# POOL drains three times inside the last stage of a transformer kernel

## The chip, the cores and the metric

The kernel runs on one core of a Trainium2 chip. The metric is the device time in microseconds (us) of one execution. The core has five engines with an instruction queue each: TensorE (PE, matmuls into PSUM), VectorE (DVE), ScalarE (ACT), GpSimd (POOL) and SyncE (SP, which here only issues DMAs). They run on their own and meet through semaphores: an instruction can raise one, and another queue can stand still until it has reached a value.

## The reference

Two layers, each with attention and a feed-forward part, over x of 4 x 512 tokens with 512 columns:

```python
x = x + _L0_xattn_ref(_layernorm(x), token_ids, ...)   # 4 experts chosen by token id
x = x + _L0_ffn_ref(_layernorm(x), norm_w, w_gv, w_out)  # quantised gated FFN, 2048 wide
x = x + _L1_xattn_ref(_layernorm(x), ctx, Wq, Wg, bg, Wkv, Wo)  # linear attention, 16 heads
x = x + _L1_ffn_ref(_layernorm(x), gate_w, w_gate, w_up, w_down, sw_gate, sw_up, sw_down)
```

The last part is a mixture of 16 experts. Each token goes to its 4 best, an expert takes at most 256 tokens, and a shared network runs for all:

```python
xg = xpad[buf]                        # 16 x 256 gathered rows
mid = silu(xg @ w_gate) * (xg @ w_up)
eout = mid @ w_down * wbuf[..., None]
y = zeros.at[buf.reshape(-1)].add(eout)[:T]
shared = silu(x @ sw_gate) * (x @ sw_up) @ sw_down
return y + shared
```

## The kernel before, in words

The kernel has two blocks. A block gives each engine its own list of instructions; at its end every engine drains and all meet in a barrier. The first block (`front_experts0`) does the first layer's attention part, the token-id experts, and ends near 235 us. The second (`ffn0_to_experts1`) does all the rest. Between and after them, the callback of `semaphores` (lines 94 and 95) clears the block's semaphores on POOL, with a drain ahead, and holds another barrier. In the profile the closing of the first block carries line 231 and that of the second line 1395.

The change touches the last part of the second block, `shared_experts1`, and there POOL's list `gpsimd`. Tokens are worked on in tiles of 128 rows and 512 columns (256 KB); an expert has two such tiles.

- POOL's `body` is called when its other work (statistics of the norms, and one half of splitting the shared network's weights, line 3629) is over. It waits for `found_ready`: DVE has then found out which token sits in which slot of which expert (`gather_idx`, `scatter_idx`, line 3989).
- `fetch(e)` issues two gathers (line 3639): 128 rows of the normed x from HBM into `xg`, by indirect DMA. TensorE transposes them.
- `add(e)` waits until the additions of the expert before have landed (`added`, lines 3644 and 3646), because two experts may add to the same row; grants ACT the other pair of output tiles (`y_free`, line 3647); then waits for each tile of `e_y` and issues a scatter that adds it to `out` in HBM (line 3651, an indirect DMA too).
- `body` runs `fetch(e + 2)` and `add(e)` for the 16 experts. It starts with `fetch(0)` and `fetch(1)` and a wait until the shared result stands in `out` (line 3660), and ends with a wait for the last additions (line 3666). Experts 14 and 15 are the last two; no fetch comes with them.
- ACT's `body` makes `e_y` from PSUM with the slots' weights (line 3746), behind waits for `y_free` and for the matmuls.
- TensorE runs each expert's matmuls in three float32r products (lines 54 to 56). SP loads the experts' weights.

POOL's DMAs of the whole kernel are: in the first block the stores of summaries (line 307) and the gathers of x (line 314), in the second the gathers by the tokens' place (line 1464), and those of lines 3639 and 3651. POOL issues them in program order, among its compute instructions.

Of the kernel before, what the change touches and what calls it, by code (L numbers as in the profile page):

```python
# [10 lines left out]
P = 128  # L11
# [756 lines left out]


def front(nc, g, io):  # L770


    ctx = ExitStack()
    with ctx:
        def sb(name, shape, dt):
            return ctx.enter_context(nc.sbuf_tensor(name, shape, dt))

        sem = semaphores(nc, ctx, "f")


        ctx_raw = sb("ctx_raw", [P, KD, S], fp32)
        ctx_h = sb("ctx_h", [P, KD, S], f32r)
        ctx_l = sb("ctx_l", [P, KD, S], f32r)
        wkv_raw = sb("wkv_raw", [P, KD, 2 * D], fp32)
        wkv_h = sb("wkv_h", [P, KD, 2 * D], f32r)
        wkv_l = sb("wkv_l", [P, KD, 2 * D], f32r)
        kneg = [sb(f"kneg{n}", [P, D], fp32) for n in range(2)]
        kexp = kneg
        kf = [sb(f"kf{n}", [P, D], fp32) for n in range(2)]
        k_h = sb("k_h", [P, 4, D], f32r)  # L790
        k_l = sb("k_l", [P, 4, D], f32r)
        v_h = sb("v_h", [P, 4, D], f32r)
        v_l = sb("v_l", [P, 4, D], f32r)
        summ = sb("summ", [P, 2, KD, P], fp32)
        summ_h = sb("summ_h", [P, 2 * KD * P], f32r)
        summ_l = sb("summ_l", [P, 2 * KD * P], f32r)
        wchunk = [sb(f"wchunk{n}", [P, 1024], fp32) for n in range(3)]
        wsum = sb("wsum", [P, 24], fp32)
        wtot = sb("wtot", [P, 2], fp32)
        wall = sb("wall", [P, 2], fp32)  # L800
        tok = sb("tok", [P, TT], i32)
        tokf = sb("tokf", [P, TT], fp32)
        ge = sb("ge", [P, TT, E0 - 1], fp32)
        mask = sb("mask", [P, TT, E0], fp32)
        mask_b = sb("mask_b", [P, TT, E0], bf16)
        tot = sb("tot", [P, TT, E0], fp32)
        rank = sb("rank", [P, TT, E0], fp32)
        inc = sb("inc", [P, TT, E0], fp32)
        cnt_i = sb("cnt_i", [P, E0], i32)
        ntile = sb("ntile", [P, E0], fp32)  # L810
        upto = sb("upto", [P, E0], fp32)
        base = sb("base", [P, E0], fp32)
        base_rows = sb("base_rows", [P, E0], fp32)
        tex = sb("tex", [1, 3, SORTED + AHEAD], fp32)
        posf = sb("posf", [P, TT], fp32)
        qi = sb("qi", [P, 2, TT], i32)
        qf = sb("qf", [P, 2, TT], fp32)

        hot_row = wkv_raw[:, 0:2, :].rearrange("p a (t n) -> p (a t) n", n=P)
        hot_tile = wkv_raw[:, 2, 0:TT * (SORTED + AHEAD)].rearrange("p (t n) -> p t n", t=TT)  # L820
        idxf = sb("idxf", [P, SORTED + AHEAD], fp32)

        s = {n: sem(n) for n in (
            "tok_in wkv_in wkv_hi wkv_lo mask_ready counted rank_read hot_ready sorted_ready route_step "
            "ctx_in ctx_hi ctx_lo ctx_kept ctx_raw_free ctx_used "
            "k_ready v_ready kbank_free vbank_free kneg_ready kexp_ready kf_ready k_hi k_lo v_hi v_lo "
            "kv_used bd_ready ks_ready summ_taken summ_ready summ_hi summ_lo summ_out "
            "wsum_ready wtot_ready wall_ready wscale_ready last_step").split()}
        w_in = [sem(f"w_in{n}") for n in range(3)]
        w_free = [sem(f"w_free{n}") for n in range(3)]  # L830

        kbank, vbank = g.bank[0:2], g.bank[2:4]
        bd_bank, ks_bank, route_bank, sort_bank = g.bank[4], g.bank[5], g.bank[6], g.bank[7]
        NJ = SORTED + AHEAD

        with nc.Block() as block:
            @block.sync
            def _(sp):
                sp.dma_start(tok[:, :], io["tokens"]).then_inc(s["tok_in"], 16)
                sp.dma_start(wkv_raw[:, :, :], io["wkv"]).then_inc(s["wkv_in"], 16)  # L840
                with sp.Fori(0, B) as b:
                    sp.wait_ge(s["ctx_raw_free"], b + 1)
                    sp.dma_start(ctx_raw[:, :, :], io["ctx"][:, bass.ds(b, 1), :, :].rearrange("p a k s -> p (a k) s")).then_inc(s["ctx_in"], 16)
                    for c in range(6):
                        sp.wait_ge(w_free[c % 3], at(b, 2, c // 3))
                        sp.dma_start(wchunk[c % 3][:, :], io["wffn"][:, bass.ds(b * 6144 + c * 1024, 1024)]).then_inc(w_in[c % 3], 16)

            @block.gpsimd
            def _(gp):
                gp.wait_ge(s["wtot_ready"], 1)  # L850
                gp.partition_all_reduce(wall[:, :], wtot[:, :], P, bass.bass_isa.ReduceOp.add).then_inc(s["wall_ready"], 1)

            @block.scalar
            def _(act):
                act.wait_ge(s["wkv_in"], 16)
                act.activation(wkv_h[:, :, :], wkv_raw[:, :, :], ACT.Copy).then_inc(s["wkv_hi"], 1)
                for n in range(3):
                    act.sem_inc(w_free[n], 1)
                with act.Fori(0, B) as b:
                    act.wait_ge(s["ctx_in"], (b + 1) * 16)  # L860
                    act.wait_ge(s["ctx_used"], b + 1)
                    act.wait_ge(s["ctx_kept"], b * 32 + 32)
                    act.activation(ctx_h[:, :, :], ctx_raw[:, :, :], ACT.Copy).then_inc(s["ctx_hi"], 1)

                    for part, mine, every in (("ctx_hi", ctx_h, g.ctx_h), ("ctx_lo", ctx_l, g.ctx_l)):
                        act.wait_ge(s[part], b + 1)
                        act.dma_start(f(every[:, bass.ds(b, 1), :].rearrange("p a n -> p (a n)")),
                                     f(mine[:, :, :].rearrange("p k n -> p (k n)"))).then_inc(s["ctx_kept"], 16)
                    for t in range(4):
                        for c in ((0, 1), (2, 3), (4,), (5,))[t]:  # L870
                            act.wait_ge(w_in[c % 3], at(b, 2, c // 3) * 16)
                            act.activation(wchunk[c % 3][:, :], wchunk[c % 3][:, :], ACT.Abs,
                                           accum_out=wsum[:, bass.ds(b * 6 + c, 1)]).then_inc(w_free[c % 3], 1)
                        if t == 0:
                            act.wait_ge(s["kv_used"], b + 1)
                        act.wait_ge(s["kneg_ready"], at(b, 4, t))
                        act.activation(kexp[t % 2][:, :], kneg[t % 2][:, :], ACT.Exp).then_inc(s["kexp_ready"], 1)
                        act.wait_ge(s["v_ready"], at(b, 4, t))
                        act.activation(v_h[:, t, :], vbank[t % 2][:, :], ACT.Copy).then_inc(s["v_hi"], 1)
                        act.wait_ge(s["kf_ready"], at(b, 4, t))  # L880
                        act.activation(k_h[:, t, :], kf[t % 2][:, :], ACT.Copy).then_inc(s["k_hi"], 1)
                    act.wait_ge(s["summ_ready"], b + 1)
                    act.wait_ge(s["summ_out"], b * 32 + 32)
                    act.activation(summ_h[:, :], summ[:, :, :, :].rearrange("p w k n -> p (w k n)"), ACT.Copy).then_inc(s["summ_hi"], 1)
                    for part, (ready, mine) in enumerate((("summ_hi", summ_h), ("summ_lo", summ_l))):
                        act.wait_ge(s[ready], b + 1)
                        act.dma_start(g.summ_dram[bass.ds(b, 1), part, :, :].rearrange("a p n -> (a p) n"), f(mine[:, :])).then_inc(s["summ_out"], 16)
                act.wait_ge(s["summ_out"], 32 * (B + 1))
                act.wait_ge(s["ctx_kept"], 32 * (B + 1))

            @block.tensor
            def _(pe):

                pe.wait_ge(s["mask_ready"], 1)
                m2 = mask_b[:, :, :].rearrange("p t e -> p (t e)")
                pe.matmul(route_bank[:, 0:TT * E0], g.before_b[:, :], m2, start=True, stop=True)
                pe.matmul(route_bank[:, 256:256 + TT * E0], g.ones_b[:, :], m2, start=True, stop=True).then_inc(s["counted"], 1)

                pe.wait_ge(s["hot_ready"], 1)
                for t in range(TT):  # L900
# [1351 lines left out]


def ffn0(nc, g, io):

    PAIRS = TT // 2
# [1928 lines left out]
```

## Time and profile before

| what | us |
|---|---|
| median of 3 runs | 1107.89 |
| lowest and highest of them | 1104.54, 1109.40 |
| the profiled execution | 1107.26 |
| its span, first to last instruction | 1105.5 |
| PE busy | 1048.1 (95%) |
| DVE busy | 673.4 (61%) |
| ACT busy | 591.9 (54%) |
| POOL busy | 281.9 (26%) |

The span is measured by the hardware profiler in one execution. Times in the views are us from the start of the span. "Busy" leaves out what an engine's sequencer does alone: semaphore waits, branches and drains. Such records carry a q behind the engine's name (POOLq). A DMA that POOL issues counts as a POOL instruction, as long as POOL works at issuing it; its landing is later.

### The profile page before, as it was taken

How to read it: one execution, taken by the hardware profiler on the slowest of the kernel's cores; microseconds unless marked ns; L12 is line 12 of the kernel's file. 1: busy time of each engine (PE TensorE's matmuls, PEld its weight loads, DVE VectorE, ACT ScalarE, POOL GpSimd, SP SyncE). 2: the span in 40 equal slices, each digit the busy share in tenths (PEclk: the TensorE clock that was granted, in tenths of full speed). 3: DMA queues.
4: the chain of work that ended last, by engine and by line, in shares of the span. 5: the costliest groups of instructions: out<-in, count | busy, mean ns of one | idle time of the engine just before them, and what ended most of it. 6: DMA issues, size and time to landing. Idle time of an engine off the chain costs nothing.

```text
span 1105.5 us, 16228 instructions
## 1 busy us (share of the span) xinstructions
PE 1048.1 (95%) x5830; PEld 824.7 (75%) x5830; DVE 673.4 (61%) x1226; ACT 591.9 (54%) x890; POOL 281.9 (26%) x445
## 2 busy tenths in 40 slices
PE   7999999979999999989999999899899999999994
PEld 5887777766455555568888888688687899999993
DVE  6746555435998998665655655466823666666660
ACT  5765787734898898853333244121113466666651
POOL 1012222113555553100000034100010044444442
PEclk9999999989999999999999999999999999999998
DMA  6682666521100000201111232302043588888853
GB/s 213 227 303 97 172 173 188 163 68 59 30 20 20 30 20 11 97 1 68 48 58 51 101 108 77 100 29 77 1 152 111 181 236 223 225 227 230 231 132 39
DMA packets 47606, 127.03 MB, mean 115 GB/s; under 512 B 5810, under 2 KB 6834, under 8 KB 46772
## 3 DMA queue, kind: packets, MB, share of 16 engines
q1 hardware_dynamic: 36516, 97.53, 26.1%
q0 software_dynamic: 10448, 27.58, 11.0%
q10 hardware_dynamic: 576, 1.05, 0.3%
q8 instruction: 40, 0.66, 0.2%
q14 instruction: 26, 0.21, 0.1%
HBM read 97.76 MB, written 28.38 MB: 114 GB/s over the span
## 4 chain that ended last, share of the span: by engine, by line
PE 67%; DVE 5%; ACT 3%; issue 2%; POOL 1%; DMA 0%; ACTq 0%; DVEq 0%; POOLq 0%
PE bank L54 16%; PE bank L55 15%; PE bank L56 15%; PE bank L1819 9%; PE bank L1840 4%; PE bank L3812 1%; PE bank L1831 1%; DVE s_hot_tile L3975 1%; PE bank L1913 1%; PE bank L1895 1%; DVE s_pick L3972 1%; PE bank L1924 1%; PE bank L1849 1%; PE bank L1923 1%; DVE s_mid L3999 0%
## 5 line engine op out<-in xcount | busy, mean ns | idle before, releaser
L1819 PE MATMUL bank<-w,f_qT 128*128 128x512 bf16 x512 | 117.9, 379 | 0.2 <-DVE f_h L2060 0.2
L3651 POOL DMA_INDIRECT out<-e_y,scatter_idx x32 | 69.0, 2157 | 115.7 <-ACT e_y L3746 111.5
L1819 PEld LDWEIGHTS bank<-w,f_qT 128*128 128x128 bf16 x512 | 48.7, 98 | 50.8 <-issue 0.6
L3688 ACT ACTIVATE s_m_h<-s_mid 128x512 fp32r<-128x512 f32 (+1 forms) x24 | 15.1, 631 | 126.9 <-DVE s_mid L3999 76.3
L3639 POOL DMA_INDIRECT e_xg<-xn_rows,gather_idx x32 | 33.7, 1054 | 172.6 <-DVE gather_idx L3989 105.7
L54 PE MATMUL bank<-wkv_h,ctx_h_all 128*128 128x512 f32 x128 | 54.0, 422 | 12.0 <-DVE wkv_l L708 7.4
L1840 PE MATMUL bank<-w,f_q2T 128*128 128x512 bf16 x256 | 59.5, 387 | 2.4 <-ACT f_q2T L1593 2.4
L54 PE MATMUL bank<-e_xT_h,e_wg_h 128*128 128x256 f32 (+1 forms) x192 | 56.5, 294 | 2.9 <-issue 2.1
L2060 DVE SCALAR_TENSOR_TENSOR f_h<-bank,f_columns,f_sg 128x512 f32<-128x512 f32 x64 | 47.9, 749 | 13.8 <-ACT f_sg L1577 6.8
L4077 DVE TENSOR_TENSOR e_mid<-bank,e_sil 128x256 f32<-128x256 f32 (+1 forms) x48 | 20.3, 423 | 55.5 <-ACT e_sil L3720 55.4
L55 PE MATMUL bank<-e_xT_l,e_wu_h 128*128 128x256 f32 (+1 forms) x192 | 54.1, 282 | 0.0
L56 PE MATMUL bank<-e_xT_h,e_wg_l 128*128 128x256 f32 (+1 forms) x192 | 54.0, 281 | 0.0
L55 PE MATMUL bank<-e_xT_l,e_wg_h 128*128 128x256 f32 (+1 forms) x192 | 54.0, 281 | 0.0
L56 PE MATMUL bank<-e_xT_h,e_wu_l 128*128 128x256 f32 (+1 forms) x192 | 54.0, 281 | 0.0
L54 PE MATMUL bank<-e_xT_h,e_wu_h 128*128 128x256 f32 (+1 forms) x192 | 54.0, 281 | 0.0
L55 PE MATMUL bank<-wkv_l,ctx_h_all 128*128 128x512 f32 x128 | 52.9, 413 | 0.0
L56 PE MATMUL bank<-wkv_h,ctx_l_all 128*128 128x512 f32 x128 | 52.6, 411 | 0.0
L1531 POOL TENSOR_TENSOR f_columns<-f_columns,minus_half 128x1 f32<-128x1 f32 x16 | 8.8, 549 | 166.0 <-DVE f_columns L2153 166.0
L1840 PEld LDWEIGHTS bank<-w,f_q2T 128*128 128x128 bf16 x256 | 25.3, 99 | 33.8 <-issue 5.2
L1577 ACT ACTIVATE f_sg<-bank,f_columns 128x512 f32<-128x512 f32 x64 | 43.7, 685 | 12.1 <-issue 6.1
L3720 ACT ACTIVATE e_sil<-bank 128x256 f32<-128x256 f32 (+1 forms) x48 | 18.4, 383 | 52.3 <-PE bank L56 52.3
L54 PEld LDWEIGHTS bank<-e_xT_h,e_wg_h 128*128 128x128 f32 (+1 forms) x192 | 34.5, 180 | 6.8 <-issue 4.6
(415 smaller groups left out, 3289.9 us busy)
## 6 DMA issues: line engine op xcount, KB each, us to landing
wraw<-in_wffn SPq DMA_DIRECT2D x48, 512.0 KB, 4.2
e_raw_g<-in_ew_gate SPq DMA_DIRECT2D x16, 704.0 KB, 4.0
e_raw_u<-in_ew_up SPq DMA_DIRECT2D x16, 704.0 KB, 5.4
e_raw_d<-in_ew_down SPq DMA_DIRECT2D x16, 512.0 KB, 6.5
sorted_y<-e_y SPq DMA_DIRECT2D x19, 256.0 KB, 4.3
x_rows<-rows SPq DMA_DIRECT2D x16, 256.0 KB, 2.0
xn_rows<-a_work SPq DMA_DIRECT2D x16, 256.0 KB, 2.0
s_raw<-x_rows SPq DMA_DIRECT2D x16, 256.0 KB, 2.7
```

Of the source, the lines that this page charges most:

```text
L54: pe.matmul(out, ah, bh, start=first, stop=False)
L55: pe.matmul(out, ah, bl, start=False, stop=False)
L56: return pe.matmul(out, al, bh, start=False, stop=last)
L1577: act.activation(sg[c % 2][:, :], gbank[c % 2][:, :], ACT.Silu, scale=deq[t % 3][:, 0:1]).then_inc(sg_ready, 1)
L1819: ins = pe.matmul(bank[c % 2][:, :], qT[t % 2][:, k * P:(k + 1) * P], w_gv(k, col + c * 512), start=(k == 0), stop=(k == KD - 1))
L1840: ins = pe.matmul(obank[:, :], q2T[:, k * P:(k + 1) * P], w_out[:, k, :], start=(k == 0), stop=(k == HID // P - 1))
L2060: v.scalar_tensor_tensor(out=h2[t % 2][:, c * 512:(c + 1) * 512], in0=vbank[c % 2][:, :], scalar=deq[t % 3][:, 0:1], in1=sg[c % 2][:, :], ...
L3639: gp.indirect_dma_start(xg[t][u][:, :], None, g.xn_dram, bass.IndirectOffsetOnAxis(g.gather_idx[:, slot:slot + 1], 0)).then_inc(e_arrived[ ...
L3651: gp.indirect_dma_start(io["out"], bass.IndirectOffsetOnAxis(g.scatter_idx[:, slot:slot + 1], 0), e_y[t][u][:, :], None, compute_op=ALU.ad ...
L3688: ins = act.activation(m[0][r, c, :], mid[n % 2][r, :], ACT.Copy)
L3720: act.activation(e_sil[n][0:r, :], hbank[n][0:r, 0:CAP], ACT.Silu).then_inc(e_sil_ready, 1)
L4077: v.tensor_tensor(e_mid[n][0:r, :], hbank[n][0:r, CAP:2 * CAP], e_sil[n][0:r, :], ALU.mult).then_inc(e_mid_ready, 1)
```

## The change

One instruction, `gp.drain()`, is put into POOL's list in two places, and is run three times: once at the start of `body`, and in `add(e)` for the last two experts, behind the wait for the additions of the expert before and ahead of the grant of `y_free`. The rest of the diff deletes functions that nothing calls (`front`, `gather_rows`, `experts0`, `there`, `ffn0`, `attention1`, `route1`, `shared1`, `experts1`), some 1,700 lines; the line numbers behind them fall.

```diff
         def add(e):
             i, u = e // 2, e % 2
             if u:
                 gp.wait_ge(added[0], (i + 1) * 32)
             elif i:
                 gp.wait_ge(added[1], i * 32)
+            if e >= E1 - 2:
+                gp.drain()
             gp.sem_inc(y_free[1 - u], 1)
             for t in range(2):
                 gp.wait_ge(e_y_ready[u], i * 2 + (t + 1))
...
         def body():
+            gp.drain()
             gp.wait_ge(found_ready, 1)
             fetch(0)
             fetch(1)
```

## Rows read from the trace of the kernel before

**Rows 1.** The page, part 1: busy us of each engine (share of the span).
```profile
PE 1048.1 (95%) x5830; PEld 824.7 (75%) x5830; DVE 673.4 (61%) x1226; ACT 591.9 (54%) x890; POOL 281.9 (26%) x445
```

**Rows 2.** Chain that ended last, its end: start us, us, what.
```profile
1090.98 0.70 ACT e_y L3746
...
1091.94 1.56 POOL out L3651
```

**Rows 3.** Busy us by engine in stretches; then TensorE clock, DMA share, GB/s.
```profile
1093.50:1097.20 3.70, 0.00 (x0) 0.00 (x0) 0.00 (x0) 0.00 (x0) 0.01 (x1) 0.78 0.73 101
1097.20:1103.80 6.60, 0.00 (x0) 0.00 (x0) 0.00 (x0) 0.00 (x0) 0.00 (x0) 0.50 0.00 0
1103.80:1105.50 1.70, 0.00 (x0) 0.00 (x0) 0.00 (x0) 0.00 (x0) 0.00 (x0) 0.50 0.00 0
```

**Rows 4.** Records of lines 3666 and 1395 on POOL's sequencer: count, ns, start us.
```profile
L3666 POOLq EVENT_SEMAPHORE  x1: 17/17/17, 1097.0 to 1097.0; - x1
...
L1395 POOLq DRAIN  x1: 6586/6586/6586, 1097.2 to 1097.2; - x1
```

**Rows 5.** Records of lines 231 and 94: ns min/median/max, first and last start.
```profile
L231 POOLq DRAIN  x1: 2285/2285/2285, 213.4 to 213.4; - x1
...
L94 POOLq DRAIN  x2: 188/233/278, 235.2 to 1104.0; - x2
```

**Rows 6.** POOL's DMAs, groups by line: count, busy us, mean ns, idle before.
```profile
L3651 POOL DMA_INDIRECT out<-e_y,scatter_idx x32 | 69.0, 2157 | 115.7 <-ACT e_y L3746 111.5 <-issue 4.3
L3639 POOL DMA_INDIRECT e_xg<-xn_rows,gather_idx x32 | 33.7, 1054 | 172.6 <-DVE gather_idx L3989 105.7 <-DMA out<-s_raw 57.7 <-issue 9.1
L314 POOL DMA_INDIRECT e_xg<-in_x,sorted_idx x19 | 19.5, 1024 | 10.7 <-DVE sorted_idx L634 7.5 <-issue 3.1
L1464 POOL DMA_INDIRECT f_x<-sorted_y,pos x16 | 17.1, 1068 | 26.1 <-POOLq L95 23.4 <-issue 2.7
...
L307 POOL DMA_DIRECT2D summaries<-summ_h x3 | 2.1, 684 | 56.7 <-ACT summ_h L355 56.7
L307 POOL DMA_DIRECT2D summaries<-summ_l x3 | 1.7, 564 | 9.0 <-DVE summ_l L658 8.8 <-issue 0.2
```

**Rows 7.** POOL's busy us and instructions in two stretches.
```profile
0.00:213.40 213.40, 41.94 (x87) 0.99 0.61 195
235.00:1097.20 862.20, 239.85 (x358) 0.99 0.33 97
```

**Rows 8.** POOL in order of time, around its long idle: start us, us.
```profile
701.15 1.26 POOL L3629 TENSOR_TENSOR s_wd_h<-s_raw,s_wd_h 64x512 fp32r<-64x512 f32 x1 [4.15 <-ACT s_wd_h L3674]
808.16 1.09 POOL L3639 DMA_INDIRECT e_xg<-xn_rows,gather_idx  x1 [105.74 <-DVE gather_idx L3989]
```

**Rows 9.** Line 3647, the grant behind a wait: expert 14 alone, then all.
```profile
L3647 POOLq EVENT_SEMAPHORE  x1: 17/17/17, 1074.1 to 1074.1; - x1
...
L3647 POOLq EVENT_SEMAPHORE  x16: 17/17/17, 871.0 to 1086.4; - x16
```

**Rows 10.** POOL in order of time, experts 13 to 15: start us, us.
```profile
1065.85 2.91 POOL L3651 DMA_INDIRECT out<-e_y,scatter_idx  x1 [6.44 <-ACT e_y L3746]
...
1079.36 1.55 POOL L3651 DMA_INDIRECT out<-e_y,scatter_idx  x1 [8.70 <-ACT e_y L3746]
1081.40 1.56 POOL L3651 DMA_INDIRECT out<-e_y,scatter_idx  x1 [0.48 <-ACT e_y L3746]
1089.93 1.55 POOL L3651 DMA_INDIRECT out<-e_y,scatter_idx  x1 [6.97 <-ACT e_y L3746]
```

**Rows 11.** ACT in order of time, first copies of experts 14 and 15.
```profile
1078.39 0.69 ACT L3746 ACTIVATE e_y<-bank,slot_weight 128x512 f32<-128x512 f32 x1 [0.86 <-PE bank L56]
...
1088.97 0.69 ACT L3746 ACTIVATE e_y<-bank,slot_weight 128x512 f32<-128x512 f32 x1 [1.57 <-PE bank L56]
```

**Rows 12.** POOL in order of time, behind the first block's end.
```profile
236.91 1.04 POOL L1464 DMA_INDIRECT f_x<-sorted_y,pos  x1 [23.36 <-POOLq L95]
238.25 0.97 POOL L1464 DMA_INDIRECT f_x<-sorted_y,pos  x1 [0.31 <-issue]
```

More of the change, by code:

```diff
@@ L1250, in there @@
-def there(t, pairs):
-    return not isinstance(t[0], int) or 0 <= t[0] < pairs
 def ffn0_to_experts1(nc, g, io):
@@ L3113, in shared1 @@
-def shared1(nc, g, io):
-    ctx = ExitStack()
-    with ctx:
-        def one(name, shape, dt):
-            return ctx.enter_context(nc.sbuf_tensor(f"s1_{name}", shape, dt))
-        def sb(name, shape, dt):
-            return [one(f"{name}{u}", shape, dt) for u in range(2)]
-        sem = semaphores(nc, ctx, "s1")
-        wg, wu, wd = g.shared_w
-        sil, mid = sb("sil", [P, S], fp32), sb("mid", [P, S], fp32)
-        m = one("m_h", [P, SFT, S], f32r), one("m_l", [P, SFT, S], f32r)
-        rows = one("rows", [P, 4, D], fp32)
-        spare = one("spare_rows", [P, D], fp32)
-        rows_in, rows_out, spare_ready, spare_out = [sem(n) for n in "rows_in rows_out spare_ready spare_out".split()]
-        g_ready, u_ready, sil_ready, mid_ready, m_hi, m_lo, o_ready, res_ready = [sem(n) for n in "g_ready u_ready sil_ready mid_ready m_hi m_lo o_ready res_ready".split()]
-        gbank, ubank, obank = g.bank[0:2], g.bank[2:4], g.bank[4:6]
-        with nc.Block() as block:
-            @block.sync
-            def _(sp):
-                sp.wait_ge(spare_ready, 1)
-                sp.dma_start(io["out"][T:T + P, :], spare[:, :]).then_inc(spare_out, 16)
-                sp.sem_inc(rows_out, 16)
-                with sp.Fori(0, B) as b:
-                    sp.wait_ge(rows_out, (b + 1) * 16)
-                    sp.dma_start(rows[:, :, :], g.x3_dram[bass.ds(b * S, S), :].rearrange("(t p) n -> p t n", p=P)).then_inc(rows_in, 16)
-                    sp.wait_ge(res_ready, at(b, 4, 3))
-                    sp.dma_start(io["out"][bass.ds(b * S, S), :].rearrange("(t p) n -> p t n", p=P), rows[:, :, :]).then_inc(rows_out, 16)
-                sp.wait_ge(rows_out, 16 * (B + 1))
-                sp.wait_ge(spare_out, 16)
-            @block.gpsimd
-            def _(gp):
-                gp.memset(spare[:, :], 0.0).then_inc(spare_ready, 1)
-            @block.scalar
-            def _(act):
-                with act.Fori(0, B) as b:
-                    for c in range(SFT):
-                        act.wait_ge(g_ready, at(b, SFT, c))
-                        act.activation(sil[c % 2][:, :], gbank[c % 2][:, :], ACT.Silu).then_inc(sil_ready, 1)
-                        act.wait_ge(mid_ready, at(b, SFT, c))
-                        act.activation(m[0][:, c, :], mid[c % 2][:, :], ACT.Copy).then_inc(m_hi, 1)
-            @block.tensor
-            def _(pe):
-                def batch(b):
-                    def xT(k):
-                        return [x[:, k, bass.ds(b * S, S)] for x in (g.xT_h, g.xT_l)]
-                    for c in range(SFT):
-                        if c >= 2:
-                            pe.wait_ge(mid_ready, at(b, SFT, c - 2))
-                        for w, bank, ready in ((wg, gbank, g_ready), (wu, ubank, u_ready)):
-                            for k in range(KD):
-                                last = mm3(pe, bank[c % 2][:, :], [x[:, k, c * P:(c + 1) * P] for x in w], xT(k), k == 0, k == KD - 1)
-                            last.then_inc(ready, 1)
-                    for t in range(4):
-                        if t >= 2:
-                            pe.wait_ge(res_ready, at(b, 4, t - 2))
-                        for c in range(SFT):
-                            if t == 0:
-                                pe.wait_ge(m_lo, at(b, SFT, c))
-                            last = mm3(pe, obank[t % 2][:, :], [x[:, c, t * P:(t + 1) * P] for x in m], [x[:, c, :] for x in wd], c == 0, c == SFT - 1)
-                        last.then_inc(o_ready, 1)
-                with pe.Fori(0, B) as b:
-                    batch(b)
-            @block.vector
-            def _(v):
-                with v.Fori(0, B) as b:
-                    for c in range(SFT):
-                        v.wait_ge(sil_ready, at(b, SFT, c))
-                        v.wait_ge(u_ready, at(b, SFT, c))
-                        v.tensor_tensor(mid[c % 2][:, :], ubank[c % 2][:, :], sil[c % 2][:, :], ALU.mult).then_inc(mid_ready, 1)
-                        v.wait_ge(m_hi, at(b, SFT, c))
-                        v.tensor_tensor(m[1][:, c, :], mid[c % 2][:, :], f(m[0][:, c, :]), ALU.subtract).then_inc(m_lo, 1)
-                    v.wait_ge(rows_in, (b + 1) * 16)
-                    for t in range(4):
-                        v.wait_ge(o_ready, at(b, 4, t))
-                        v.tensor_tensor(rows[:, t, :], obank[t % 2][:, :], rows[:, t, :], ALU.add).then_inc(res_ready, 1)
```

1357 lines of the change are left out of this document (removed).

## The prediction

> **What bounds the kernel now.** I read the page first. TensorE is busy 95% of the span [rows 1], and the change touches no instruction of it, so nothing of that 95% can move unless POOL makes it wait. POOL is busy 26%. The second thing to read is the end, because a change on POOL can only pay where POOL is what ends last. In the chain that ended last, the last matmul is followed by the ACT copy of `e_y` and the last POOL scatter, issued at 1091.94 and over at 1093.50 [rows 2]; the span is 1105.5. So 12.0 us follow the last busy instruction of any engine. In the table of stretches [rows 3] they fall into three: 3.7 us in which the DMA engines work (share 0.73), then 6.6 us in which every engine and the DMA engines stand at 0.00, then 1.7 us. The records of line 1395, the closing of the block, say what the empty 6.6 us are: one DRAIN on POOL's sequencer, started at 1097.2 and 6586 ns long [rows 4]. It isn't waiting for a transfer: POOL's wait for the last additions to land had passed at 1097.0 [rows 4], and the DMA share is 0.00. It is work of its own, and all of it is on the path.
>
> **What sets the length of that drain.** The profile has other POOL drains [rows 5]. The one that closes the first block, line 231, took 2285 ns. Those of line 94, which each follow a block's drain with no DMA between, took 188 and 278 ns. Since the start POOL had then issued 6 + 19 = 25 DMAs (lines 307 and 314, the page's list by line [rows 6]); between that drain and the last one it issued 16 + 32 + 32 = 80 (lines 1464, 3639, 3651). A straight line through both: (6586 - 2285) / (80 - 25) = 78 ns for each DMA, and 2285 - 25 x 78 = 0.33 us with none, close to the 0.19 and 0.28 us seen with none. I take it that a POOL drain clears what was issued since the drain before it, at 78 ns per DMA on a floor of 0.33 us. Two other measures fit less well but lead to the same place. By POOL instructions, 87 and 358 in the two stretches [rows 7], it is 16 ns each on a floor of 0.90 us; the floor is off from 0.19 to 0.28. By time, 213 and 862 us, it is 6.6 ns per us on 0.87 us, off in the same way. In all three a drain behind a recent drain is short.
>
> The Trainium skill (VectorE: DVE Perf Modes, section The DRAIN you can't avoid) knows a DRAIN of the preamble and postamble of about 12 ns, constant, on all five engines. [...]
>
> **The change, part by part.** The long diff deletes functions that nothing calls; no instruction comes or goes with them. It costs nothing, and the line numbers alone move. Three instructions are added, all drains on POOL.
>
> *Drain 1, ahead of the routed experts* (line 3655, before the wait for `found_ready`). POOL ends its last subtraction at 702.41 and issues its next DMA at 808.16, idle for 105.74 us until DVE has `gather_idx` [rows 8]. 16 DMAs since the first block's drain: 0.33 + 16 x 0.078 = 1.6 us. Bounds: 0.19 us (line 94) and 6.6 us (the longest drain there is). Cost 0 either way; the cover is DVE's search for the slots, and only a drain over 105 us would lose it.
>
> *Drain 2, in add(14)*, after the wait for the additions of expert 13, which passes at 1074.1 [rows 9]. Behind it on POOL are the grant of `y_free[1]`, and the two scatters of expert 14. 32 gathers and 28 scatters have been issued since drain 1, so 0.33 + 60 x 0.078 = 5.0 us; bounds 0.19 and 6.6 us. It ends near 1079.1. The scatter needs `e_y`, which ACT ends at 1078.39 + 0.69 = 1079.08, and it started at 1079.36 [rows 10, 11]. So it fits to a few tenths. A lateness there isn't yet a loss: the scatters of expert 14 are over at 1082.96, have landed at 1086.4, and nobody needs that before ACT's `e_y` of expert 15 at 1088.97 + 0.69 = 1089.66 [rows 9 to 11]. ACT's own wait for `y_free[1]` comes only there. Cost 0, with 3.3 us to spare.
>
> *Drain 3, in add(15)*, at 1086.4. Two DMAs since drain 2: 0.33 + 0.16 = 0.5 us, bounds 0.19 and 6.6. Behind it stands the last pair of scatters, due at 1089.66. It ends near 1086.9. Cost 0, and 2.8 us remain. Above 3.3 us it would lengthen the kernel by the excess.
>
> *The last drain*, line 1395, is not edited but has 2 DMAs (expert 15) to clear in place of 80: 0.49 us in place of 6.59, a gain of 6.1 us. Bounds of the new length: 0.28 us (line 94 right behind it, nothing between) and 0.90 us (the floor by instructions), so a gain of 5.7 to 6.3 us. Nothing is late next: no other engine has work left in that stretch [rows 3], and the 1.7 us behind it stay.
>
> *The first scatter behind a drain.* This price the trace does not show. A scatter that follows a gather takes 2.91 us (expert 13's first), one that follows a scatter 1.55 us (the firsts of experts 14 and 15), even after 8.7 us of idleness [rows 10]. So something of a scatter is prepared anew, for 1.36 us, when another kind of POOL work has come between; a drain might count as such. A gather pays less: the first behind the drains at the first block's end took 1.04 us, its successor 0.97 [rows 12]; the first behind compute [rows 8] took 1.09. Bounds: 0, and 1.36 us. I take 0, since the drains ahead of rows 12 left a gather no dearer than ordinary compute did. At expert 14 even 1.36 us is hidden in the 2.8 us. At expert 15 it isn't: of 1.36 us, 0.16 go into the 0.46 us gap before the second scatter, which could be 0.30, so 1.2 us reach the end.
>
> **The sum.** The profiled execution took 1107.26 us, 1.76 more than its span of 1105.5: 1107.26 - 6.1 = 1101.2. The median of the three shown runs is 0.63 higher, 1107.89; against it the same gain gives 1101.8. I take 1101.2.
>
> **The rivals.**
>
> *The drain displaces the scatter's preparation.* For it: gathers do so for 1.36 us [rows 10]. Against it: the cheap gather behind drains [rows 12]. The gain shrinks to 6.1 - 1.2 = 4.9 us: 1102.4.
>
> *The last drain stays long.* The drain inside the body only waits for POOL to be done, while the one at the block's end does a walk of its own over whatever the block issued. For it: the only long drains seen close a block. Against it: the drain of line 94 is also part of a closing, is short right behind a long one, and so sees that its predecessor has cleared. Three short drains are hidden, the last stays at 6.59: 1107.3. [...]
>
> *Slower: each drain costs the full price.* If the length isn't counted from the drain before but over the whole kernel, drain 2 takes up to 6.6 us and ends at 1080.7, 1.6 late; expert 14's scatters land near 1088.0; drain 3 ends at 1094.6, 4.9 us after `e_y` is ready; and the last one stays. 1107.26 + 4.9 = 1112.2, and 1113.4 if the scatter is also prepared anew. It decides from the point where drain 3 exceeds 3.3 us. For it: a count over the whole kernel also makes the last drain longer than line 231's. Against it: 0.19 and 0.28 us at line 94 [rows 5].
>
> **How the numbers follow.** Chances: forecast 0.68, scatter prepared anew 0.16, last drain stays long 0.11, each at full price 0.05. A measurement of this kernel can tell about 0.5%, 5.5 us, from no change. The forecast's 6.1 us (0.55%) is barely past that, and the three runs shown lie 4.9 us apart, so I count seven tenths of the forecast and a fifth of the second case as faster by over 0.5%: 0.48 + 0.03 = 0.51. Slower by over 0.5% is the fourth case in part, with a little for scatter of the runs: 0.03. The rest, 0.46, lies within 0.5%. Range: down from 1101.2 by 2.7, as the lowest of the three runs lies 3.35 under their median and a median strays less; up to 1105.0, that is the second case's 1102.4, plus 0.6 for the median's offset, 1.5 for the highest run above it, and 0.5 for the drain's floor. What is left out are the last two cases and a little scatter.
>
> **What would show it right or wrong.** Right: POOL drains of about 1.6, 5.0 and 0.5 us at the added lines, and one of about 0.5 us closing the block; a span near 1099.4. The second near 3.3 us would speak for time, or 1.9 us (0.90 + 61 x 0.016) for instructions. The first scatter of expert 15 at 1.55 us supports the forecast, at 2.9 us the first rival. A last drain still at 6.6 us is the second rival; a third drain over 3.3 us the third. The prediction is wrong in its root if the drains of the body come out short and the last one stays.

## The result and the profile after

| | before | after |
|---|---|---|
| median of six runs each, us | 1107.62 | 1099.75 |
| lowest and highest | 1104.54, 1109.40 | 1098.41, 1102.43 |
| profiled execution, its span | 1107.26, 1105.5 | 1101.63, 1099.8 |

The ratio is 0.994 with a 95% interval of 0.9924 to 0.9956, so between 4.9 and 8.4 us less. The median lies inside the forecast's range, 1.5 us below its 1101.2. Timed a second time beside the experiments, the change came out at 0.9952 (0.9933 to 0.9971), 3.2 to 7.4 us less. Both intervals hold the 6.4 us that the trace accounts for.

The records of the drains in the profile after. The line numbers are new: 1979 is the drain at the start of `body`, 1970 that in `add` (experts 14 and 15), 1991 the last wait, 910 the block's close (1395 before). Columns as in rows 4 and 5.

```profile
L1979 POOLq DRAIN  x1: 2632/2632/2632, 703.3 to 703.3; - x1
L1970 POOLq DRAIN  x2: 201/2576/4952, 1074.8 to 1087.5; - x2
L1991 POOLq EVENT_SEMAPHORE  x1: 17/17/17, 1097.7 to 1097.7; - x1
L910 POOLq DRAIN  x1: 201/201/201, 1097.9 to 1097.9; - x1
```

The last drain is 201 ns where it was 6586 [rows 4]. The rest of the closing is as it was: line 94's drains read 188/233/278 again, as in rows 5. Three stretches of the tail, which answer to rows 3 (columns as there):

```profile
1094.06:1097.70 3.64, 0.00 (x0) 0.00 (x0) 0.00 (x0) 0.00 (x0) 0.01 (x1) 0.71 0.75 103
1097.90:1098.10 0.20, 0.00 (x0) 0.00 (x0) 0.00 (x0) 0.00 (x0) 0.00 (x0) 0.50 0.00 0
1098.20:1099.80 1.60, 0.00 (x0) 0.00 (x0) 0.00 (x0) 0.00 (x0) 0.00 (x0) 0.50 0.00 0
```

The last landing ends at the wait: 3.6 us here, 3.5 before (from 1093.50 to 1097.0, the wait of rows 4). The closing behind the last drain takes 1.7 us in both (1098.12 to 1099.81, and 1103.80 to 1105.48), and between the two 0.2 us have taken the place of 6.6. POOL in order of time at experts 13 to 15, which answers to rows 10, and ACT's first and last copies of `e_y` (rows 11):

```profile
1066.41 2.91 POOL L1975 DMA_INDIRECT out<-e_y,scatter_idx  x1 [6.47 <-ACT e_y L2071]
1069.63 1.60 POOL L1975 DMA_INDIRECT out<-e_y,scatter_idx  x1 [0.30 <-issue]
1080.50 1.56 POOL L1975 DMA_INDIRECT out<-e_y,scatter_idx  x1 [9.28 <-ACT e_y L2071]
1082.36 1.57 POOL L1975 DMA_INDIRECT out<-e_y,scatter_idx  x1 [0.30 <-issue]
1090.51 1.55 POOL L1975 DMA_INDIRECT out<-e_y,scatter_idx  x1 [6.58 <-ACT e_y L2071]
1092.50 1.56 POOL L1975 DMA_INDIRECT out<-e_y,scatter_idx  x1 [0.45 <-ACT e_y L2071]
```

```profile
1078.95 0.69 ACT L2071 ACTIVATE e_y<-bank,slot_weight 128x512 f32<-128x512 f32 x1 [0.86 <-PE bank L56]
...
1089.54 0.69 ACT L2071 ACTIVATE e_y<-bank,slot_weight 128x512 f32<-128x512 f32 x1 [1.58 <-PE bank L56]
1091.54 0.69 ACT L2071 ACTIVATE e_y<-bank,slot_weight 128x512 f32<-128x512 f32 x1 [1.31 <-PE bank L56]
```

Expert 14's first `e_y` is ready at 1079.64 and its scatter starts at 1080.50, 0.86 us later where it was 0.28. The drain ahead of it ended at 1074.8 + 4.95 = 1079.75, only 0.11 us behind `e_y`; but from the end of that drain to the scatter another 0.75 us pass, where 0.28 us pass from `e_y` to a scatter otherwise. Together this holds the scatter up by 0.58 us. The prediction had no term for the 0.75 us. Expert 15's starts 0.28 us behind its `e_y` (1090.23 to 1090.51), as before (1089.65 to 1089.93): nothing of the delay has got through. From the end of the last `e_y` to the end of the span there are now 1099.8 - 1092.24 = 7.6 us, and there were 1105.5 - 1091.68 = 13.8. That difference, 6.2 us, is the change: 6.4 us of drain, less some 0.1 us by which the last landing took longer. The last `e_y` itself was 0.56 us later in this execution than before, and 2.1 us earlier than before in the repeated one, whose tail was 7.4 us. So what lies ahead of the tail differs by 2.7 us between two executions of one kernel, and the tail by 0.2. Among the twelve timed executions of the repeated run the shortest, 1098.39 us, had a mean granted TensorE clock of 0.994 of the full one, the longest, 1105.49 us, one of 0.983. So the medians, 7.9 us apart, do not show a gain beyond the 6.4; where their other 1.5 us lie, no run shows.

### The profile page after: what moved, and what is told of

Same layout as the page of the kernel before. It is cut to its first block, busy times and chain, and to the rows that moved or that the text cites. A ratio compares the mean times of both kernels' runs of the same rounds, so it can differ in the third digit from the quotient of the medians.

```text
span 1099.8 us, 16229 instructions
## 1 busy us (share of the span) xinstructions
PE 1046.3 (95%) x5830; PEld 824.2 (75%) x5830; DVE 673.4 (61%) x1226; ACT 592.3 (54%) x890; POOL 282.5 (26%) x445
## 4 chain that ended last, share of the span: by engine, by line
PE 67%; DVE 5%; ACT 2%; issue 2%; POOL 1%; DMA 0%; ACTq 0%; DVEq 0%; POOLq 0%
PE bank L54 16%; PE bank L56 15%; PE bank L55 15%; PE bank L1334 9%; PE bank L1355 4%; PE bank L2137 1%; PE bank L1346 1%; DVE s_hot_tile L2300 1%; PE bank L1428 1%; PE bank L1410 1%; DVE s_pick L2297 1%; PE bank L1439 1%; PE bank L1364 1%; PE bank L1438 1%; PE bank L2111 0%
## 5 line engine op out<-in xcount | busy, mean ns | idle before, releaser
L1153 ACT ACTIVATE a_th<-bank 128x512 f32<-128x512 f32 x16 | 9.5, 597 | 56.0 <-PE bank L1391 56.0
```

## Experiments

All start from the changed kernel. Where no ratio is given, the kernel was timed once, and only its trace is used. A first reading of its trace corrected the price list used in the expectations. The drains of 60 and of 2 DMAs took 4952 and 201 ns: (4952 - 201) / 58 = 82 ns per DMA, on 0.201 - 2 x 0.082 = 0.04 us. The one with 16 DMAs took 2632 ns instead of 1.35 us, but started at 703.3, when POOL's last subtraction, here in its timeline (start us, us), had just begun and had 1.2 us to run:

```profile
703.25 1.26 POOL L1951 TENSOR_TENSOR s_wd_h<-s_raw,s_wd_h 64x512 fp32r<-64x512 f32 x1 [4.15 <-ACT s_wd_h L1999]
```

**The change again, and the drain where it has no cover.**

> The changed kernel itself, timed again beside the others. The theory, as corrected by its first trace: a POOL drain takes 0.04 us, plus 0.082 us for each DMA that POOL has issued since the drain before it, plus what is left of the compute instruction that is still running. The last drain falls from 6.59 to 0.20 us and nothing else changes: 6.4 us faster than the kernel before, ratio 0.9942. If the medians seen first (7.9 us apart) hold, something beyond the last drain has got faster: ratio near 0.993.

Measured: 0.9952 (0.9933 to 0.9971), drains of 2627, 4952, 201 and 201 ns. The theory's 0.9942 lies in the interval, and 0.993 just outside, too close for the total alone to separate; the tails do it (13.8 against 7.6 and 7.4 us).

```diff
-            if e >= E1 - 2:
+            if e == E1 - 1:
                 gp.drain()
...
         def body():
-            gp.drain()
             gp.wait_ge(found_ready, 1)
```

> Only the drain in the addition of expert 15 is left. Theory: it has 78 DMAs to clear, 0.04 + 78 x 0.082 = 6.4 us, and begins 3.3 us before the first e_y of expert 15 is ready, so the first scatter starts about 3.1 us late, and the last drain takes 0.20 us: net gain 6.4 - 3.1 = 3.3 us, ratio 0.997. A theory in which the drain's work is hidden wherever it stands ahead of the last scatters expects the full 6.4 us, ratio 0.994. If each drain pays the full price whatever came before, both drains take 6.5 us and the kernel is 3.1 us slower, ratio 1.003.

Measured: 0.9984 (0.9966 to 1.0001). The drains, then POOL at expert 15 and ACT's first copy for it:

```profile
L1970 POOLq DRAIN  x1: 6427/6427/6427, 1085.8 to 1085.8; - x1
L910 POOLq DRAIN  x1: 206/206/206, 1100.3 to 1100.3; - x1
```

```profile
1093.03 1.55 POOL L1975 DMA_INDIRECT out<-e_y,scatter_idx  x1 [10.61 <-issue]
1094.89 1.57 POOL L1975 DMA_INDIRECT out<-e_y,scatter_idx  x1 [0.31 <-issue]
```

```profile
1088.43 0.69 ACT L2070 ACTIVATE e_y<-bank,slot_weight 128x512 f32<-128x512 f32 x1 [1.57 <-PE bank L56]
```

The 6.43 us are those of 78 DMAs. `e_y` is ready at 1089.12, the scatter starts at 1093.03, 3.91 us later where 0.28 is usual: the wait in POOL is no longer named after ACT but "issue", that is, POOL itself. The first scatter is 3.6 us late and not 3.1: the drain ends at 1085.85 + 6.43 = 1092.28, 3.16 us behind `e_y`, and the 0.75 us from a drain's end to the scatter come on top, in place of 0.28. The second, which used to wait for its own `e_y`, is 3.5 us late. The net gain is 6.4 - 3.5 = 2.9 us (0.9974), inside the interval. A drain keeps its length wherever it stands; the change gains because its long drains stand in gaps. The theory of the hidden drain anywhere (0.994) is out, and so is the one in which each pays the full price.

**More DMAs, no added drain.** 32 small direct DMAs ahead of the experts, all three drains removed:

```diff
             fetch(1)
+            gp.wait_ge(spare_out, 16)
+            for n in range(32):
+                gp.dma_start(spare[:, n * 16:(n + 1) * 16], g.xn_dram[0:P, n * 16:(n + 1) * 16]).then_inc(extra, 16)
...
                 add(e)
+            gp.wait_ge(extra, 512)
```

> No drain is added; instead POOL issues 32 small direct DMAs (128 rows of 64 bytes from the normed rows into a scratch tile) in its idle time ahead of the routed experts. They add nothing to the output. Theory: the last drain grows by 32 x 0.082 = 2.6 us to 9.2 us, and the kernel is 2.6 us slower. If the drain's length counts POOL's instructions (16 ns each), it grows by 0.5 us to 7.1 us. If it counts only indirect DMAs, or time, it stays at 6.6 us.

```profile
L910 POOLq DRAIN  x1: 7088/7088/7088, 1099.1 to 1099.1; - x1
```

The theory missed: 7.09 us, not 9.2. The number is that of the rival by instructions, and equally that of (7.09 - 0.04) / 0.082 = 86 DMAs. The time, 1.000 (0.9979 to 1.002), can't tell 0.5 from 2 us. It does show that the gain is not the deleted functions': they are gone here too, and without the added drains so are the 6.4 us. The next experiment separates these: both batches stand in the idle time after the first four gathers, in the changed kernel.

```diff
+            gp.wait_ge(spare_out, 16)
+            for n in range(32):
+                gp.dma_start(spare[:, n * 16:(n + 1) * 16], g.xn_dram[0:P, n * 16:(n + 1) * 16]).then_inc(extra, 16)
+            gp.wait_ge(extra, 512)
+            gp.drain()
+            for n in range(8):
+                gp.dma_start(spare[:, :], g.xn_dram[0:P, :]).then_inc(extra, 16)
+                gp.wait_ge(extra, 512 + 16 * (n + 1))
+            gp.drain()
```

> The changed kernel, with 32 small DMAs (128 rows of 64 bytes) and then 8 large ones (128 rows of 2 KB) issued by POOL into a scratch tile in its idle time, a drain behind each batch once it has landed; they add nothing to the output. The batch of small ones comes after 4 gathers. If a small DMA has a lower price in a drain than a large one (16 ns, as the 0.50 us for 32 of them suggest), the first of the two drains takes 0.04 + 4 x 0.082 + 32 x 0.016 = 0.88 us. If each DMA costs 0.082 us and only a limited number, about 86, can stand to be cleared, it takes 0.04 + 36 x 0.082 = 3.0 us. The second takes 0.04 + 8 x 0.082 = 0.70 us in either case. The drains of the change keep their lengths, but for the one at expert 14, which loses the 4 gathers already cleared: 4.6 us.

```profile
L1988 POOLq DRAIN  x1: 2994/2994/2994, 831.6 to 831.6; - x1
L1992 POOLq DRAIN  x1: 691/691/691, 863.6 to 863.6; - x1
L1971 POOLq DRAIN  x2: 201/2410/4618, 1073.2 to 1086.0; - x2
```

36 DMAs, 32 of them small, take 2.99 us: a DMA of 64-byte rows costs a drain as much as one of 2 KB rows, and the rival by instructions (0.90 + 36 x 0.016 = 1.5 us) or by size is out. So if the price held in the run before too, its last drain did not pay for 26 of the 112 DMAs. Is 86 a limit of the count?

```diff
         def body():
             gp.drain()
+            gp.wait_ge(spare_out, 16)
+            for n in range(96):
+                at_ = (n % 64) * 8
+                if n == 64:
+                    gp.wait_ge(extra, 64 * 16)
+                gp.dma_start(spare[:, at_:at_ + 8], g.xn_dram[0:P, at_:at_ + 8]).then_inc(extra, 16)
+            gp.wait_ge(extra, 96 * 16)
+            gp.drain()
             gp.wait_ge(found_ready, 1)
```

> The changed kernel with 96 small DMAs (128 rows of 32 bytes) issued by POOL between its first drain and the wait for the slots, and a drain behind them once they have landed; all of it in the 105 us in which POOL is idle, and nothing of it reaches the output. If a drain never clears more than about 86 DMAs, whatever their size, this one takes 0.04 + 86 x 0.082 = 7.1 us. If the 86 of the earlier run was a matter of what its DMAs were, this drain clears all 96: 7.9 us. The four drains behind it keep 4.95, 0.20, 0.20 us, and the time stays that of the change.

```profile
L1988 POOLq DRAIN  x1: 7894/7894/7894, 758.6 to 758.6; - x1
```

All 96 are paid, 0.04 + 96 x 0.082 = 7.91. It isn't a limit of the count of DMAs; a limit on something else is not ruled out. What relieved the last drain of 26 in the mix of small DMAs, gathers and scatters stays open; it doesn't touch the change, since all 80 of the kernel before counted.

**Which of the three drains does what.** The first alone (the two lines in `add` removed):

> Only the drain ahead of the routed experts is left. Theory: it takes 2.6 us (16 DMAs, 1.35 us, after 1.2 us of waiting for the subtraction still running), and the last drain has 64 DMAs, 0.04 + 64 x 0.082 = 5.3 us. If any earlier drain in the block were enough, the last would take 0.2 us; if the count went by POOL's instructions (65 since then, 16 ns each on 0.9 us), 1.9 us; if nothing but the block's whole count mattered, 6.6 us.

```profile
L1977 POOLq DRAIN  x1: 2626/2626/2626, 705.1 to 705.1; - x1
L910 POOLq DRAIN  x1: 5278/5278/5278, 1099.3 to 1099.3; - x1
```

5.28 us are 64 DMAs. An earlier drain takes off exactly what was issued up to it, no more. The other two without the first (its line removed):

> The drain ahead of the routed experts is left out, the two others stay. Theory: the one in the addition of expert 14 has 76 DMAs, 6.3 us in place of 4.95; expert 14's first scatter starts about 0.9 us later than in the changed kernel, which the slack before expert 15's scatters hides; the third and the last drain stay at 0.20 us, so the tail is as short as in the changed kernel. If the first drain is needed, the scatters of expert 15 start late behind their e_y.

```profile
L1970 POOLq DRAIN  x2: 206/3235/6264, 1074.3 to 1088.6; - x2
L910 POOLq DRAIN  x1: 201/201/201, 1097.2 to 1097.2; - x1
```

```profile
1081.30 1.56 POOL L1975 DMA_INDIRECT out<-e_y,scatter_idx  x1 [10.60 <-ACT e_y L2070]
1083.16 1.57 POOL L1975 DMA_INDIRECT out<-e_y,scatter_idx  x1 [0.30 <-issue]
1089.97 1.55 POOL L1975 DMA_INDIRECT out<-e_y,scatter_idx  x1 [5.24 <-ACT e_y L2070]
```

Expert 14's first `e_y` was ready at 1079.12, so its scatter, 2.18 us behind it, is 1.9 us late against the usual 0.28. That is 1.3 us more than in the change, where 0.9 had been expected: the drain is 1.3 us longer, and it held the scatter up in the change already. But expert 15's starts at 1089.97, 0.28 us behind its `e_y` at 1089.69. The slack takes it all, and the tail is 7.4 us. The first drain isn't needed. Nor, nearly, is the third: only `if e == E1 - 2: gp.drain()` left:

> One drain in place of three, in the addition of expert 14. Theory: it has 76 DMAs, 6.26 us, starts the scatters of expert 14 about 0.9 us late, which is hidden, and leaves 4 DMAs for the last drain, 0.37 us. Gain 6.2 us against the kernel before, ratio 0.9944, 0.17 us behind the change. If the first or third drain is needed to keep the middle one hidden, the scatters of expert 15 come late and the gain falls by as much.

```profile
L1970 POOLq DRAIN  x1: 6264/6264/6264, 1074.0 to 1074.0; - x1
L910 POOLq DRAIN  x1: 369/369/369, 1096.7 to 1096.7; - x1
```

Measured 0.995 (0.9927 to 0.9972), not to be told from the change. Expert 14's first scatter was 2.1 us late (1080.98, `e_y` ready at 1078.63), not 0.9, and hidden all the same. By the trace one drain carries the gain but for 0.17 us (0.37 in place of 0.20).

**What a drain waits for besides.** The first drain behind `gp.wait_ge(found_ready, 1)` instead of ahead of it:

> The first drain stands behind the wait for the slots instead of ahead of it, so POOL's last subtraction is long over when it begins. Theory: its 2.63 us were 1.24 us of waiting for that subtraction and 1.36 us for 16 DMAs, so now 1.36 us. If the 2.63 us were due to the many POOL instructions or the long time since the drain before, it stays near 2.6 us.

```profile
L1980 POOLq DRAIN  x1: 1362/1362/1362, 809.2 to 809.2; - x1
```

1.36 us for 16 DMAs, after a hundred idle microseconds more. By POOL's 294 instructions since the first block it would be 0.90 + 294 x 0.016 = 5.6 us, by the time gone by 0.87 + 573 x 0.0066 = 4.7 us; neither counts. The other 1.27 us of the drain in its first place are accounted for by the subtraction, which had 1.2 us to run. Next, one more `gp.drain()` right behind the last two scatters:

> The changed kernel with one more drain right behind the last two scatters, ahead of the wait for their landing. If a POOL drain waits for the DMAs in flight, it lasts until they land, about 3.6 us, and the closing drain finds nothing to clear: 0.04 us in place of 0.20. If it only counts what was issued, it takes 0.20 us at once.

```profile
L1990 POOLq DRAIN  x1: 5277/5277/5277, 1092.0 to 1092.0; - x1
L1992 POOLq EVENT_SEMAPHORE  x1: 17/17/17, 1097.3 to 1097.3; - x1
L910 POOLq DRAIN  x1: 53/53/53, 1097.5 to 1097.5; - x1
```

It starts before the last scatter is issued (at 1092.20, 1.56 us long) and ends at 1097.2; that scatter landed 4.9 us after 1092.20, at 1097.1, and the wait behind the drain passes at once. So a POOL drain also waits for what is in flight. The 3.6 us of the expectation left out the 1.8 us until the issue was over. The drain with nothing left takes 0.05 us. And a drain at every expert (`if e >= 1:` in place of `if e >= E1 - 2:`):

> The drain ahead of the routed experts stays, and one stands in the addition of every expert from 1 to 15. Theory: 10 DMAs for the first of them (0.86 us), 4 for most (two gathers, two scatters: 0.37 us), 2 for the last two (0.20 us); all hidden. The first scatter of an expert from 1 to 13 still takes 2.9 us, because the gathers came between, and 1.55 us for experts 14 and 15: the drain neither adds nor takes this. If a drain displaced what a scatter needs, experts 14 and 15 would show 2.9 us. If a drain has a price of its own above 1 us, each of the 15 shows it.

The whole line, then the one at expert 13 alone, then POOL around it:

```profile
L1970 POOLq DRAIN  x15: 201/2336/3508, 892.0 to 1085.8; - x15
...
L1970 POOLq DRAIN  x1: 2336/2336/2336, 1059.3 to 1059.3; - x1
```

```profile
1057.80 0.98 POOL L1961 DMA_INDIRECT e_xg<-xn_rows,gather_idx  x1 [0.30 <-issue]
1065.22 2.90 POOL L1975 DMA_INDIRECT out<-e_y,scatter_idx  x1 [6.45 <-ACT e_y L2071]
1068.43 1.60 POOL L1975 DMA_INDIRECT out<-e_y,scatter_idx  x1 [0.30 <-issue]
1078.72 1.55 POOL L1975 DMA_INDIRECT out<-e_y,scatter_idx  x1 [8.69 <-ACT e_y L2071]
```

The sizes missed: 1.7 to 3.5 us in place of 0.4 to 0.9, for the drains of experts 1 to 13. They come 1.5 to 2.2 us behind the start of a gather and wait for it. At expert 13 it took 3.65 us to land, at 1057.80 + 3.65 = 1061.45, and the drain ended at 1059.31 + 2.34 = 1061.65. For all twelve experts from 2 to 13 the trace has this end 0.20 us behind the landing (0.45 at expert 1), although 4 DMAs had been issued and would cost 0.37: part of the clearing seems to fit into the wait. The two drains with no gather ahead are 0.20 us. The scatters answer the other question: 2.9 us where a gather came between, drain or not, and 1.55 us behind a drain alone.

## Why the prediction was right

*That the last drain clears what was issued since the drain before it* was right, and is shown by ten drains on one line, 0.04 + 0.082 n us:

| DMAs n | line, us | measured, us |
|---|---|---|
| 4 | 0.37 | 0.369 |
| 8 | 0.70 | 0.691 |
| 16 | 1.35 | 1.362 |
| 36 | 2.99 | 2.994 |
| 56 | 4.63 | 4.618 |
| 64 | 5.29 | 5.278 |
| 76 | 6.27 | 6.264 |
| 78 | 6.44 | 6.427 |
| 80 | 6.60 | 6.586 |
| 96 | 7.91 | 7.894 |

(Two more, of 60 and of 2 DMAs, made the line.) The two other measures weighed are ruled out: the drain moved behind its wait would have taken 5.6 us by instructions and 4.7 by time, and took 1.36; the last drain of the run with the first alone would have taken 1.9 and 3.5, and took 5.28. What no run separates is a price for each DMA from one for each row, since every DMA of POOL in these runs has 128 rows.

*The term that was mis-sized is the floor.* 78 ns on 0.33 us should have been 82 ns on 0.04. What was wrong there is taking line 231's 2285 ns as clearing alone: it starts at 213.40, while POOL's last compute instruction of the first block still runs, and so holds 0.14 us of that. POOL's timeline of the kernel before:

```profile
213.28 0.26 POOL L323 TENSOR_SCALAR e_shift<-e_mv,e_rstd 128x1 f32<-128x1 f32 x1
```

Of the 2.285 us, 0.04 + 25 x 0.082 = 2.09 are clearing and 213.28 + 0.26 - 213.40 = 0.14 are this; the remaining 0.05 no run explains. The last drain was 0.20 and not 0.49 us, below the lower bound of 0.28; the gain 6.4 and not 6.1 us. That bound, and the support of the floor of 0.33, came from line 94's drains with no DMA ahead of them, 0.19 and 0.28 us, which the law of 0.04 us does not cover. Line 95 has the other drains with none, and they fit it:

```profile
L95 POOLq DRAIN  x2: 40/43/46, 236.0 to 1105.2; - x2
```

What line 94's drains hold beyond 0.04 us stays open; they have the same length in the kernel before and after.

*Drain 1* was put at 1.6 us and took 2.63: the same omission, with 1.27 us of a running subtraction. The 105 us of idleness hid it, as forecast, and the run without it shows that it wasn't needed. *Drain 2*, 5.0 against 4.95, held up the scatter of expert 14 by 0.58 us, without effect. The forecast's fit "to a few tenths" was right for the drain's end, but left out the 0.47 us that a scatter starts later behind a drain (0.75) than behind its `e_y` (0.28). *Drain 3*, 0.5 against 0.20, was hidden. For the same reason the point from which a drain there is exposed is not 3.3 but 2.8 us: 6.43 us made the scatter 3.6 us late. It didn't matter to a drain of 0.20 us.

*The first rival*, a drain that displaces what a scatter needs, is out: 1.55 us behind a drain in the change and in the run with 15 drains. *The second*, a last drain that stays long, is out by 201 against 6586 ns. The Trainium skill (VectorE: DVE Perf Modes, section The DRAIN you can't avoid) gives its constant of about 12 ns for the drains that the runtime puts into a program's preamble and postamble. Lines 231 and 1395 are drains of the kernel's own blocks, so the page says nothing on them, and no run here tests it. *The third* is out by the same rows. The forecast time came 1.5 us above the median and 0.4 us below the profiled run. The term in the tail was 0.3 us too small; the closeness beyond that is luck, since what lies ahead of the tail moves by more from run to run.

## What to carry to other kernels

Look at what the closing of a block does, not only at the last busy instruction: here 6.6 us in which nothing was busy were one engine's drain, paying for each of the 80 DMAs that it had issued in the block. Such a debt can be paid early, in a gap of that engine that is longer than the debt, behind the landing of its last DMA and after most of them have been issued; one drain in the right gap is enough. In a gap that is too short the excess comes back at full price, and here the scatter behind it started 0.75 us after the drain's end.

## What the runs showed of the hardware

A drain on POOL took 0.04 us plus 0.082 us for each DMA issued since the drain before, each of 128 rows, the same in mixes of gathers and scatters that add, and for direct DMAs with rows of 32 or 64 bytes (0.082) or 2 KB (0.081). It also waited for a running compute instruction (1.27 us) and for DMAs in flight (5.28 us, until the last scatter had landed). With no DMA it took 0.04 to 0.05 us, but 0.19 and 0.28 us at line 94; why is open. A scatter whose `e_y` was ready by then started 0.75 us after the drain's end (1079.75 to 1080.50). With 112 DMAs of mixed kinds its length was that of 86 (7.09 us), with 96 small ones that of all (7.89 us); why is open. A scatter with addition takes 1.35 us longer to issue when a gather was issued before it (2.90 against 1.55 us), and a drain between them changes nothing.
